# Three expert layers in batches of four blocks, two of them with the inverse root kept by token columns

## The chip, the cores and the metric

The kernel runs on one core of a Trainium2 chip, alone. The metric is the device time of one execution in microseconds (us). The engines are named as in the profile: PE is the matrix engine (PEld is its weight loads), DVE the vector engine, ACT the scalar engine, POOL is GpSimd, and SP is the engine whose queue issues the DMAs here.

## The reference, cut to what matters

Four layers, each a mixing step followed by a mixture of experts with a residual. The mixing steps (attention, similarity, a state-space scan, involution) are outside the change. The expert step of the first and the third layer is, for the tokens `t` of 64 channels (8 images of 1024 tokens), with two experts a token (`TOP_K = 2`):

```python
t = t + _L0_ffn_ref(_ln_t(t), ...)          # _ln_t: (v - mean) / sqrt(var + 1e-5) over the channels
...
gate_logits = xf @ Wg + bg                  # xf: the tokens, normalised; 8 experts
top_w, top_i = jax.lax.top_k(gate_logits, TOP_K)
top_w = jax.nn.softmax(top_w, axis=-1)
w_dense = jnp.sum(jax.nn.one_hot(top_i, E, dtype=xf.dtype) * top_w[..., None], axis=1)
for e in range(E):
    h = jax.nn.gelu(xf @ W1[e] + b1[e], approximate=False)
    out = out + w_dense[:, e:e + 1] * (h @ W2[e] + b2[e])
```

In the first, third and fourth layer (the last one) W1 is 64x256 and W2 256x64 for each expert; in the second layer the hidden size is 128. Everything is float32. All experts are computed for all tokens, and the gates that are 0 take out what isn't wanted.

## The kernel before

**Layout.** Images go in pairs: the 128 partitions hold 64 channels of two images, the columns 4 x 1024 tokens. `X` is the residual. A tile is 512 of these columns, so an expert step has `NT = 8` tiles, and it is one program block that begins when all engines have left the block before. `HIDDEN` gives 2 blocks of 128 hidden units per expert in layers L0, L2 and L3 and 1 in L1; so a tile has 16 blocks in those three. `experts("L0")` and `experts("L2")` have `norms=1` (the layer norm is made inside), `experts("L3")` has `norms=0` (the normalised input and the router's input come by DMA), and so has L1.

**A block on PE.** `up(t, k, b)` (L654) is two matmuls, one for each image half: 64 rows of weights by 128 columns, 512 tokens. The two use different row halves of the array. ACT then makes `Gelu` of both halves in one instruction (L734). `down(b)` (L666) is two matmuls of 128 rows by 64 columns into the two partition halves of one PSUM bank; the two blocks of an expert accumulate. The trace shows each float32 matmul as two records, with two weight loads.

**The order.** In a round PE goes up for two blocks and then down for the two blocks before them: 8 rounds a tile. Four PSUM banks take what goes up, two (4 and 5) the experts' outputs in turn, and bank `SIDE = 7` takes the preparation of the next tile. DVE adds the bias and multiplies each expert's output by its gate row `WB` (L869), POOL adds the eight up (L585), and DVE folds the sum into `X` (L877).

**Preparation of the next tile** runs beside these rounds, at places given by the tables `pe_at`, `act_at` and `dve_at`. For `norms=1`: PE centers the tile (L604), DVE copies it to `CEN` (L768), ACT squares it (L704), PE averages the squares over channels, one matmul that leaves the variance repeated on all rows (L610). DVE then finds the inverse root on all 512 columns, by an integer guess (L778, L780) and three Newton steps of three instructions (L784 to L786), and multiplies `CEN` by it (L789). PE forms the logits from the normalised tile, four matmuls with 128 tokens as the weights and 16 output columns (L620). DVE ranks them (L797 to L811), ACT bends the difference (L712), DVE makes the gates (L830 to L834), PE turns them (L630), ACT copies the rows (L719), and SP writes them to DRAM (L547) and reads them back repeated over the partitions into `WB` (L555). The first tile of a layer has no rounds to run beside: there the whole chain stands ahead.

On PE and ACT, six of the eight tiles are run by a hardware loop and the last two are written out; DVE has the same loop, POOL loops over all eight.

## Time and profile before

| | before |
|---|---|
| time, median of 3 runs | 2050.46 us (2049.69 to 2051.26) |
| the profiled execution | 2050.83 us |
| its span, first to last instruction | 2049.0 us |
| PE busy | 1743.1 us, 85% of the span |
| DVE busy | 1056.1 us, 52% |
| ACT busy | 887.8 us, 43% |
| POOL busy | 517.9 us, 25% |

The expert blocks of the three layers lie, by the records of their first and last instructions, at about 153.8 to 446.7 us (L0), 1302.0 to 1597.0 us (L2) and 1769.1 to 2036.9 us (L3). In a timeline, records that follow each other and are alike are merged into one row with their count. The end of a matmul is modelled, so the start of the next row tells more of PE's pace than a row's own length. The number behind "PEclk" is the granted TensorE clock as a share of 2.4 GHz.

### The profile page before, as it was taken

To read this page: it belongs to the slowest core of one execution; us is meant where nothing else is said; L and a number is where in the kernel's file an instruction comes from. 1 tells how busy PE (TensorE), PEld (TensorE's weight loads), DVE (VectorE), ACT (ScalarE), POOL (GpSimd) and SP (SyncE) were. 2 spreads that over 40 slices of the span, in tenths; PEclk is the share of its full clock that TensorE was granted. 3 is DMA by queue.
4 is the path that set the end of the run, shared out by engine and by line. 5 is a ranking of instruction groups with operands and counts; after the bars stand their busy time and mean duration, and the time that the engine had idled before them with its cause. 6 is when DMAs were issued, how large, how long until landed. Compare 5 with 4: busy or idle time off the path is not lost. (4 is left out here: it accounts for less than half of the span.)

```text
span 2049.0 us, 51344 instructions
## 1 busy us (share of the span) xinstructions
PE 1743.1 (85%) x20852; PEld 761.9 (37%) x20852; DVE 1056.1 (52%) x2060; ACT 887.8 (43%) x1134; POOL 517.9 (25%) x692
## 2 busy tenths in 40 slices
PE   5777999997999788887688887699999587699997
PEld 2442333333433222233477773233333233233332
DVE  2446575733555466440276773576765276243341
ACT  3213555553435344443344434355555500555553
POOL 0001232320000134420266560122222155022222
PEclk8998999997999899998899997799999898799998
DMA  6001313110000344336433422023222030223323
GB/s 225 12 10 42 84 42 83 42 42 31 11 0 1 88 110 105 73 114 220 165 104 100 128 73 93 22 62 71 54 62 64 0 41 1 62 69 88 92 64 83
DMA packets 62287, 145.08 MB, mean 71 GB/s; under 512 B 35240, under 2 KB 35240, under 8 KB 57984
## 3 DMA queue, kind: packets, MB, share of 16 engines
q1 hardware_dynamic: 62208, 144.12, 26.3%
q8 instruction: 38, 0.62, 0.1%
q14 instruction: 41, 0.34, 0.1%
HBM read 106.07 MB, written 25.44 MB: 64 GB/s over the span
## 5 line engine op out<-in xcount | busy, mean ns | idle before, releaser
L734 ACT ACTIVATE ARENA<-PS,W 128x1024 f32<-128x1024 f32 x448 | 474.8, 1109 | 332.6 <-PE PS L654 332.3
L585 POOL TENSOR_TENSOR ARENA<-ARENA 128x512 f32<-128x512 f32 x224 | 293.0, 1308 | 1176.5 <-DVE ARENA L869 1173.3
L654 PE MATMUL PS<-ARENA,W 64*128 64x512 f32 x1792 | 463.2, 637 | 0.8 <-ACT ARENA L734 0.8
L666 PE MATMUL PS<-ARENA,W 128*64 128x512 f32 x1792 | 433.7, 605 | 12.1 <-DVE ARENA L869 12.1
L869 DVE SCALAR_TENSOR_TENSOR ARENA<-PS,W,ARENA 128x512 f32<-128x512 f32 x256 | 190.4, 750 | 341.5 <-PE PS L666 280.5
L654 PEld LDWEIGHTS PS<-ARENA,W 64*128 64x128 f32 x1792 | 160.0, 193 | 262.0 <-issue 152.7
L666 PEld LDWEIGHTS PS<-ARENA,W 128*64 128x64 f32 x1792 | 108.9, 136 | 301.9 <-issue 207.3
L1769 PE MATMUL PS<-ARENA 32*32 32x32 f32 x8448 | 106.4, 196 | 6.3 <-issue 5.9
L1246 DVE TENSOR_TENSOR ARENA<-ARENA 128x1024 f32<-128x1024 f32 x64 | 75.5, 1221 | 69.3 <-PE PS L1179 36.1
L1216 ACT ACTIVATE ARENA<-PS 128x1024 f32<-128x1024 f32 x64 | 62.0, 1021 | 93.1 <-PE PS L1169 93.1
L1769 PEld LDWEIGHTS PS<-ARENA 32*32 32x32 f32 x8448 | 95.3, 105 | 10.5 <-issue 7.1
L2000 PE MATMUL PS<-ARENA,W 128*128 x144 | 73.3, 657 | 22.2 <-DVE ARENA L2027 15.1
L1636 ACT ACTIVATE ARENA<-PS 128x512 f32<-128x512 f32 x64 | 38.2, 597 | 108.1 <-PE PS L1743 108.1
L1169 PE MATMUL PS<-ARENA 64*128 64x512 f32 x256 | 74.6, 656 | 9.1 <-DVE ARENA L1237 4.7
L1396 PE MATMUL PS<-XN,ARENA 64*128 64x512 f32 (+2 forms) x288 | 67.8, 627 | 16.7 <-ACT ARENA L1427 14.1
L1179 PE MATMUL PS<-ARENA 128*64 128x512 f32 x256 | 73.8, 606 | 4.1 <-DVE ARENA L1246 4.1
L2051 POOL TENSOR_TENSOR ARENA<-ARENA 128x512 f32<-128x512 f32 x40 | 56.4, 1411 | 58.3 <-DVE ARENA L2027 56.4
L1668 DVE STREAM_TRANSPOSE ARENA<-ARENA 128x256 f32<-128x256 f32 x64 | 28.0, 438 | 83.4 <-PEq L1336 80.3
L620 PE MATMUL PS<-W,ARENA 128*128 128x16 f32 x256 | 37.7, 281 | 34.8 <-DVE ARENA L789 18.1
L342 PE MATMUL PS<-X,W 128*128 128x512 f32 x80 | 42.7, 639 | 28.6 <-PEq L296 16.0
L1699 DVE TENSOR_TENSOR ARENA<-ARENA,PS 128x512 f32<-128x512 f32 x64 | 43.9, 686 | 41.0 <-PE PS L1769 40.6
L785 DVE SCALAR_TENSOR_TENSOR ARENA<-ARENA 128x512 f32<-128x512 f32 x48 | 59.7, 1244 | 1.6
(216 smaller groups left out, 2096.4 us busy)
## 6 DMA issues: line engine op xcount, KB each, us to landing
ARENA<-scratch_g SPq DMA_DIRECT2D x64, 768.0 KB, 9.7
ARENA<-scratch_g SPq DMA_DIRECT2D x64, 256.0 KB, 3.9
W<-w_dram SPq DMA_DIRECT2D x1, 7307.5 KB, 30.0
ARENA<-XN SPq DMA_DIRECT2D x12, 512.0 KB, 3.5
ARENA<-XN SPq DMA_DIRECT2D x16, 256.0 KB, 2.3
scratch_x<-ARENA SPq DMA_DIRECT2D x8, 512.0 KB, 4.2
scratch_b<-ARENA SPq DMA_DIRECT2D x8, 512.0 KB, 3.2
scratch_z<-ARENA SPq DMA_DIRECT2D x8, 512.0 KB, 3.8
```

The lines of the kernel that those rows point to most:

```text
L585: nc.gpsimd.tensor_tensor(SUM[:, k, :], SUM[:, k, :], TMP[:, e % 2, :], ALU.add)\
L654: last = mm(PS[:, (b % 2) * R + r, :], w(layer + "_w1", b * 128, (b + 1) * 128, half(r)), XE[half(r), k, :], start=True, stop=True)
L666: last = mm(PS[half(r), 4 + e % 2, :], w(layer + "_w2", b * C, (b + 1) * C), H[:, b % 4, r * T:(r + 1) * T], start=part == 0, stop=part == ...
L734: f(H[:, b % 4, :], PS[:, (b % 2) * R:(b % 2) * R + R, :].rearrange("p a b -> p (a b)"), ACT.Gelu, bias=w(layer + "_b1", b, b + 1)).then_i ...
L869: v.scalar_tensor_tensor(TMP[:, e % 2, :] if e else SUM[:, k, :], PS[:, 4 + e % 2, :], w(layer + "_b2", e, e + 1), WB[:, k, e, :], ALU.add ...
L1169: last = mm(PS[:, 2 * r + h, :], XH[half(r), k, m * TOK:(m + 1) * TOK], XH[half(r), k, h * T:(h + 1) * T], start=True, stop=True)
L1179: last = mm(PS[half(r), 6 + h, :], TT[k][:, r, m, :], R2[:, r, h * T:(h + 1) * T], start=m == 0, stop=m == JS - 1)
L1216: nc.scalar.activation(RL[:, r, :], both(2 * r), ACT.Relu).then_inc(s_relu.sem, 1)
L1246: v.tensor_tensor(R2[:, r, :], RL[:, r, :], RL[:, r, :], ALU.mult)\
L1396: last = mm(PS[:, 4 * (u % 2) + 2 * r + h, skip:], wt, XN[half(r), q * S + h * T + skip - back:q * S + (h + 1) * T - back], start=tap == T ...
L1769: last = mm(PS[g, MIX + k, t], XD[g, k, j, u * CHUNK:(u + 1) * CHUNK], M[g, k, u * P + j * CHUNK:u * P + (j + 1) * CHUNK], start=u == 0, s ...
L2000: nc.tensor.matmul(PS[:, n % 6, :], w("i_ws", tap * P, (tap + 1) * P), RN[:, bass.ds(q * S + h * T, T)], start=True, stop=True)\
```

## The change

`deep_experts` takes the place of `experts` in L0, L2 and L3. L1 keeps the old function. What it does otherwise:

- **Batches.** PE goes up for four blocks, then down for the four before them: 4 rounds a tile. Three pairs of PSUM banks take what goes up (`UPS = 3`), so the fourth block of a batch waits for the `Gelu` of the first. `H` has six places (`HS = 6`), so the third and fourth `Gelu` of a batch wait for an expert's output of the batch before.
- **Banks.** The other two banks are shared in turn by the experts' outputs and the preparation's steps, in the order of the list `order`; `out_of` gives the bank, and `behind` and `emptied` the wait for the one that had it before.
- **Logits.** In L0 and L2 they are formed from the centered tile `CEN`, before it is scaled (L1043), and multiplied by the inverse root on DVE (L1226), with the bias added after (L1228).
- **Inverse root.** The squares are averaged with 128 tokens as the weights and two output columns, four matmuls (L1050), so that the variance stands as 128x8. All of the root's instructions are 128x8. ACT spreads it to 128x512 (`widen`, L1150), and PE turns it to rows by the identity, four matmuls of 128x128 (`scale`, L1058). DVE multiplies `CEN` by that out of PSUM (L1233).
- **Start.** In the first tile PE goes up for four blocks, not two, ahead of the turn of the gates.
- **No loop on PE and ACT.** All eight tiles are written out there. DVE's and POOL's loops are as before. The gates' rows lie in another buffer.

```diff
+        def deep_experts(layer, norms=1, router=None):
...
+            BAT, UPS, HS = 4, 3, 6
+            XS, H = a.take(2, T), a.take(HS, R * T)
...
+            RT = ROWS[:, 0:2 * T].rearrange("p (k t) -> p k t", k=2)
...
+            VAR, INV, NEWT = (a.take(GR) for _ in range(3))
+            WIDE = a.take(G, P)
...
+                order = ["center", 0, 1, "logits", 2, 3, "scale", 4, 5, "turn", 6, 7]
+                after_scale = {0: 0, 2: 2, 4: 4, 6: 6, "center": -1, "logits": 1, "scale": 3, "turn": 5}
+                at_last = {3: 1, 5: 3, 7: 5}
+                pe_at = {0: "center", 0.5: "logits", 2: "scale", 3: "turn"}
+                act_at = {(0, 1): "square", (1, 1): "widen", (2, 1): "bend", (3, 1): "rows"}
+                dve_at = {-1: "keep", 1: "invert", 3: "rank norm", 4: "weigh"}
+            else:
+                order = [0, 1, "logits", 2, 3, 4, 5, "turn", 6, 7]
...
+                pe_at = {1: "logits", 3: "turn"}
+                act_at = {(1, 3): "bend", (3, 1): "rows"}
+                dve_at = {1: "rank", 3: "weigh"}
+
+            def out_of(unit):
+
+                return UPS * R + order.index(unit) % 2
...
+                            for g in range(G):
+                                last = mm(PS[:, out_of("logits"), GR * E + g * R:GR * E + (g + 1) * R],
+                                          SQ[:, g * TOK:(g + 1) * TOK], w("mean64")[:, 0:P:C], start=True, stop=True)
+                            last.then_inc(ln_varied.sem, 1)
+
+                    def scale(p):
+                        behind("scale", p - 1)
+                        pe.wait_ge(ln_log.sem, ln_log.at(p + 1))
+                        for g in range(G):
+                            last = mm(PS[:, out_of("scale"), g * TOK:(g + 1) * TOK],
+                                      WIDE[:, g, :], w("ident"), start=True, stop=True)
+                        last.then_inc(ln_scaled.sem, 1)
...
+                        if u >= UPS:
+                            pe.wait_ge(e_gelu.sem, e_gelu.at(u - UPS + 1))
...
+                        elif norms and e == 5:
+                            pe.wait_ge(ln_normed.sem, ln_normed.at(t + 2))
...
+                    for t in range(NT):
+                        for n in range(NBAT):
+                            for u in range(t * NB + (n + 1) * BAT, t * NB + (n + 2) * BAT):
+                                if u < NT * NB:
+                                    up(u)
+                            if t + 1 < NT:
+                                prepare(pe_at.get(n), t + 1)
+                            for b in range(n * BAT, (n + 1) * BAT):
+                                down(t, b)
...
+                        f(WIDE.rearrange("p g (r c) -> p (g r) c", r=R), INV.unsqueeze(2).to_broadcast([P, GR, C]),
+                          ACT.Copy).then_inc(ln_log.sem, 1)
...
+                        if u >= HS:
+                            act.wait_ge(e_out.sem, e_out.at((u - HS) // blocks + 1))
...
-        experts("L0")
+        deep_experts("L0")
...
-        experts("L2")
+        deep_experts("L2")
...
-        experts("L3", norms=0, router=once)
+        deep_experts("L3", norms=0, router=once)
```

PE in L0, before, the start of a looped tile: L654 goes up, L666 down, L604 centers, L610 averages the squares. `x2` counts two instructions in a row.

```order
 L604 MATMUL PS<-X,W 128x512
 L663 ISA
 L666 MATMUL PS<-ARENA,W 64x512 [waits e_gelu,e_scaled]
 L666 MATMUL PS<-ARENA,W 64x512
 L666 MATMUL PS<-ARENA,W 64x512 [waits e_gelu]
 L666 MATMUL PS<-ARENA,W 64x512
 L652 REGISTER_ALU
 L654 MATMUL PS<-ARENA,W 128x512 [waits e_gelu]
 L654 MATMUL PS<-ARENA,W 128x512
```

There are four matmuls (two blocks) between one change of kind and the next.

PE in L0, after, the third batch of the first tile: L1087 goes up (the last block of four is shown), L1058 is `scale`, L1115 goes down.

```order
 L1087 MATMUL PS<-ARENA,W 128x512 [waits e_gelu]
 L1087 MATMUL PS<-ARENA,W 128x512
 L1058 MATMUL PS<-W,ARENA 128x128 [waits ln_log,e_scaled]
 L1058 MATMUL PS<-W,ARENA 128x128 x3
 L1115 MATMUL PS<-ARENA,W 64x512 [waits e_gelu,e_scaled]
 L1115 MATMUL PS<-ARENA,W 64x512
 L1115 MATMUL PS<-ARENA,W 64x512 [waits e_gelu]
 L1115 MATMUL PS<-ARENA,W 64x512
 L1115 MATMUL PS<-ARENA,W 64x512 [waits e_gelu,ln_normed]
 L1115 MATMUL PS<-ARENA,W 64x512
 L1115 MATMUL PS<-ARENA,W 64x512 [waits e_gelu]
 L1115 MATMUL PS<-ARENA,W 64x512
```

There are eight matmuls of a kind in a row, the turned root stands between the batches, and the sixth expert (its first matmul waits for `ln_normed`) stands behind DVE's reading of it.

DVE in L0, after, the chain ahead of the first tile (rows of the ranking left out): L1204 copies the centered tile, L1211 to L1220 find the root, L1226 and L1228 take the logits, L1249 begins the ranking, L1256 ends it, L1233 is the normalised tile.

```order
 L1204 COPY ARENA<-PS 128x512 [waits ln_centered]
 L1211 TENSOR_SCALAR ARENA<-PS,W 128x8 [waits ln_varied]
 L1214 TENSOR_SCALAR ARENA<-ARENA 128x8 [waits ln_taken]
 L1215 TENSOR_SCALAR ARENA<-ARENA 128x8 [waits ln_newton]
 L1218 TENSOR_TENSOR ARENA<-ARENA 128x8 [waits ln_newton]
 L1219 SCALAR_TENSOR_TENSOR ARENA<-ARENA 128x8 [waits ln_newton]
...
 L1226 TENSOR_TENSOR ARENA<-PS,ARENA 128x64 [waits g_logits,ln_newton]
 L1228 TENSOR_TENSOR ARENA<-ARENA,W 128x64 [waits g_chain]
...
 L1256 TENSOR_TENSOR ARENA<-ARENA 128x8 [waits g_chain]
 L1233 TENSOR_TENSOR ARENA<-PS,ARENA 128x512 [waits g_chain,ln_scaled]
 L1265 TENSOR_SCALAR ARENA<-ARENA 128x8 [waits g_bent]
```

Before, the root's twelve instructions here were 128x512, and the normalised tile came ahead of the logits and the ranking; now it comes after the ranking.

## Rows read from the trace of the kernel before

**Rows 1.** Busy time by stretch, L0: PE, PEld, DVE, ACT, POOL; then PEclk, DMA

```profile
211.40:383.60 172.20, 172.15 (x742) 58.30 (x740) 116.21 (x205) 91.82 (x96) 47.65 (x35) 1.00 0.28 62
```

**Rows 2.** Timeline of PE, L0, one looped tile: start, length, line and work

```profile
279.70 1.13 PE L604 MATMUL PS<-X,W 128*128 x2
280.75 1.94 PE L666 MATMUL PS<-ARENA,W 128*64 128x512 f32 x8
282.62 1.99 PE L654 MATMUL PS<-ARENA,W 64*128 64x512 f32 x8
284.54 1.13 PE L610 MATMUL PS<-ARENA,W 128*128 128x512 f32 x2
...
298.82 1.06 PE L620 MATMUL PS<-W,ARENA 128*128 128x16 f32 x8
299.81 1.99 PE L654 MATMUL PS<-ARENA,W 64*128 64x512 f32 x8
...
307.45 1.05 PE L630 MATMUL PS<-W,ARENA 128*16 128x128 f32 x8
```

**Rows 3.** Timeline of PE, the end of L0: four blocks down in a row

```profile
440.12 3.65 PE L666 MATMUL PS<-ARENA,W 128*64 128x512 f32 x16
```

**Rows 4.** Timeline of DVE, L0: the folds of a looped and a written-out tile

```profile
383.64 0.69 DVE L877 TENSOR_TENSOR X<-X,ARENA 128x512 f32 x1 [1.57 <-POOL ARENA L585]
417.81 0.69 DVE L877 TENSOR_TENSOR X<-X,ARENA 128x512 f32<-128x512 f32 x1 [1.46 <-POOL ARENA L585]
```

**Rows 5.** Timeline of PE, linear attention: 128 weight columns, 64 moving

```profile
66.78 1.11 PE L994 MATMUL PS<-W,ARENA 128*128 128x64 f32 x8
```

**Rows 6.** Timeline of ACT, L0: two Gelus behind the up at 282.62

```profile
283.80 2.12 ACT L734 ACTIVATE ARENA<-PS,W 128x1024 f32<-128x1024 f32 x2 [1.53 <-PE PS L654]
```

**Rows 7.** Timeline of DVE, L0: one instruction of the ranking, beside POOL's addition

```profile
300.43 1.28 DVE L803 TENSOR_TENSOR ARENA<-ARENA 128x64 f32<-128x64 f32 x1
```

**Rows 8.** Timeline of PE, the start of L0

```profile
153.80 1.10 PE L604 MATMUL PS<-X,W 128*128 128x512 f32 x2 [1.12 <-PEq L920]
...
168.31 3.79 PE L654 MATMUL PS<-ARENA,W 64*128 64x512 f32 x8
173.29 1.05 PE L630 MATMUL PS<-W,ARENA 128*16 128x128 f32 x8 [1.19 <-DVEq L836]
```

**Rows 9.** Timeline of DVE, the start of L0

```profile
154.94 0.69 DVE L768 COPY ARENA<-PS 128x512 f32<-128x512 f32 x1 [1.46 <-PE PS L604]
...
168.68 0.22 DVE L802 TENSOR_REDUCE ARENA<-ARENA 128x8 f32<-128x64 f32 x1
...
171.51 0.17 DVE L811 TENSOR_TENSOR ARENA<-ARENA 128x8 f32<-128x8 f32 x1
172.02 0.17 DVE L830 TENSOR_SCALAR ARENA<-ARENA 128x8 f32<-128x8 f32 x1 [0.34 <-ACT ARENA L712]
172.23 0.17 DVE L831 TENSOR_SCALAR ARENA<-ARENA 128x8 f32<-128x8 f32 x1
...
181.53 0.75 DVE L869 SCALAR_TENSOR_TENSOR ARENA<-PS,W,ARENA 128x512 f32<-128x512 f32 x1 [3.49 <-DMA ARENA<-scratch_g]
```

**Rows 10.** Busy time by stretch, starts of L0 and L2, to read the PEclk

```profile
159.00:160.00 1.00, 0.00 (x0) 0.00 (x0) 0.93 (x3) 0.00 (x0) 0.00 (x0) 0.50 0.00 0
172.00:173.00 1.00, 0.10 (x2) 0.00 (x0) 0.84 (x5) 1.00 (x2) 0.00 (x0) 0.80 0.00 0
...
1326.00:1327.00 1.00, 1.00 (x5) 0.30 (x2) 0.00 (x0) 0.85 (x2) 0.00 (x0) 0.95 0.05 20
```

**Rows 11.** Timeline of PE, the start of L2: the turn

```profile
1321.53 1.89 PE L630 MATMUL PS<-W,ARENA 128*16 128x128 f32 x8 [1.19 <-DVEq L836]
```

**Rows 12.** Timeline of PE, the start of L3: the turn

```profile
1775.86 1.89 PE L630 MATMUL PS<-W,ARENA 128*16 128x128 f32 x8 [1.19 <-DVEq L836]
```

**Rows 13.** Timeline of DVE, L3: the third expert of the first tile

```profile
1793.46 0.75 DVE L869 SCALAR_TENSOR_TENSOR ARENA<-PS,W,ARENA 128x512 f32<-128x512 f32 x1 [5.06 <-DMA ARENA<-scratch_g]
```

**Rows 14.** DMA issues, 150 to 260 us: count, KB each, median us to landing

```profile
scratch_g<-ARENA SPq DMA_DIRECT2D x3, 32.0 KB, 1.6
```

317 lines of the change are left out of this document (added).

## The prediction

> **What bounds the kernel now.** I read the busy time by stretch first. In L0's steady part PE is busy for 172.15 of 172.20 us at the full clock, while DVE has 116 and ACT 92 [rows 1]. So a tile costs what PE issues in it. L2 and L3 show the same picture. A faster root on DVE is worth nothing there by itself; what PE does is what counts, and DVE counts only at a layer's start, where nothing runs beside its chain.
>
> The timeline of PE gives the price list, taken from one row's start to the next [rows 2]. Two blocks down take 282.62 - 280.75 = 1.87 us. Two blocks up take 284.54 - 282.62 = 1.92. Centering takes 1.05, the average of squares is as long a row (1.13) and so takes 1.05, the logits 299.81 - 298.82 = 0.99, and the turn, as long as the logits less 0.01, 0.98. A round is 3.79, and a tile is 8 x 3.79 + 1.05 + 1.05 + 0.99 + 0.98 = 34.39 us. In L3, without the two norm steps, it is 32.29.
>
> Then one row at the end of L0, where nothing is left to go up: four blocks down in a row are 3.65 us long, and a row of two is 1.94 [rows 2, 3]. So two blocks behind others of their kind cost 1.71. The rest, 0.16 down and 1.92 - 1.71 = 0.21 up, is paid for each change of kind on PE. This is the time that the batches attack.
>
> **The rounds (gain 35.5 us).** In a layer there are 64 pairs of blocks up and 64 down. In batches of four, 32 pairs of each direction stand behind a pair of their kind: 32 x 0.21 + 32 x 0.16 = 11.8 us (the pair that already did so at the end stays). Three layers give 35.5 us. A batch round is then 2 x (3.79 - 0.185) = 7.21 us.
>
> **PE's steps beside them (loss 11.5 us).** In L0 and L2, for each of 7 tiles that are prepared beside rounds:
> - the average of squares goes: -1.05;
> - eight-record group of variance matmuls comes, with 128 weight columns and 2 moving ones. The logits' group has the same weights and 16 moving columns and takes 0.99 [rows 2]. It stands directly behind the logits, so one change of kind (0.16) is not paid again: +0.83;
> - the turned root comes, four float32 matmuls with 128 weight columns and 128 moving. No row of before has both. From below, the turn with 16 weight columns takes 0.98. A row with 128 weight columns and 64 moving is 1.11 long, or 1.04 without the 0.07 by which rows overrun the next start [rows 2, 5]. From above, were the load not hidden behind the stream at all, each of 8 records would cost up to 0.99/8 = 0.12 more, 2.0 in all. I take 1.04, since that row has half the stream and the full load and shows no sum of the two.
>
> The net is +0.82 a tile, 14 tiles, 11.5 us. A tile of L0 or L2 is then 4 x 7.21 + 1.05 + 0.99 + 0.83 + 1.04 + 0.98 = 33.7 us, against 34.4. A tile of L3 is 28.84 + 0.99 + 0.98 = 30.8, against 32.3.
>
> On that last term the Trainium skill speaks against the change: "TensorE: Matmul & The Clock Gate", section "Part 3: Packing small matmuls — row/col tiling", says that a weight load overlaps a running matmul only where its row group differs. All eight records of the turned root use all rows, so by that rule the term is 2.0 and not 1.04. That is a rival below.
>
> **The start of L0 (gain 2.8).** Before, the centering starts at 153.80 and the turn of the gates at 173.29, with two blocks up behind it [rows 8]. Now, by the same rows: `CEN` is there at 154.94 + 0.69 = 155.63 [rows 9]. Logits and then variances follow on PE (0.99 + 0.83) to 157.6, with ACT's squares hidden beside the logits. Twelve instructions of 128x8 at 0.21 (172.23 - 172.02) take 2.5, and two of 128x64 for the logits 0.5: 160.8. The twelve of the ranking stay 3.0 (168.68 to 171.68): 163.8. The normalised tile comes only then, 0.7: 164.5. ACT's spreading and PE's turned root fit under the ranking. Four blocks up follow. Two took 3.79 at half the clock [rows 8]; four take 3.79 + 3.42 - 0.1 = 7.1, so the turn starts at about 171.7. The gates (1.2 us of DVE from 164.5) are long done. That is 1.6 us earlier, with one pair more behind it, worth 1.71: 3.3 us.
>
> The clock takes some of it. It fell to 0.50 in the idle of the root and rose again around 172.2, before the turn [rows 10]. The turn now starts before that moment, 0.5 us of it at half: 2.8 remain. If the clock does not fall in the shorter idle (4 us and 2 us instead of 9), the four blocks take 3.6 and 3.5 us more are gained, in each of L0 and L2. If it rises 3 us later, 1.5 are lost.
>
> **The starts of L2 (gain 2.5) and L3 (gain 0.9).** L2 is the same chain, but there the turn itself ran at half the clock, 1.89, and the clock rose only at about 1326.05 [rows 10, 11]. With the turn 1.6 us earlier that much more runs at half: 3.3 - 0.8. In L3 the logits chain does not change, and the first two blocks up were hidden behind the ranking; four are 7.1 us, from 1770.9 to 1778.0, where the turn started at 1775.86 [rows 12]. That is -2.1, +1.71 for the pair, and +1.3 since less work at half the clock is left behind the turn.
>
> **What the gates' trip does.** The first scaling waited for the DMA until 181.53, 6.5 us behind the rows of gates, and in L3 the third expert's until 1793.46, 15.1 us behind them [rows 9, 13]. Both are measured from the turn, which moves by -1.6 and +2.1. Behind the turn PE now has 3.6 (up) + 1.05 + 1.8 before the first output and 3.6 + 1.05 + 3.6 before the logits, the first step that waits for the first scaling. In L0 that is 172.9 + 8.3 = 181.2 against 173.7 + 6.5 + 0.75 = 181.0. It just fits; if it does not, it is some tenths, once a layer.
>
> **The new waits, at nothing.** (a) The fourth block up waits for the first's `Gelu`. A `Gelu` starts 283.80 - 282.62 = 1.18 us after the batch and is 1.11 long [rows 2, 6]: 2.29, and the fourth block starts at 0.2 + 3 x 0.855 = 2.77. Cover 0.5 us, less the semaphore. Behind that wait on PE stand the whole preparation and the downs. (b) `Gelu`s three and four wait for an output of the batch before; they end 2.4 us after it, and the block that needs the fourth starts 1.7 + 0.2 + 1.7 = 3.6 after it. (c) The sixth expert waits for the normalised tile. From the end of the fourth expert: DVE scales it (0.9), ranks (3.0), loses about 1.05 where POOL's addition holds one instruction (0.22 becomes 1.28 [rows 7]) and normalises (0.75): 5.7 to 5.9. PE: 3.6 + 1.04 + 1.71 = 6.4. Cover 0.5. (d) Written-out code: the fold of the first written-out tile comes 34.17 us after the one before [rows 4], no slower than the 34.39 of the sum, so it costs nothing there, on either engine.
>
> **Sum.** 35.5 - 11.5 + 2.8 + 2.5 + 0.9 = 30.2 us. The profiled execution took 2050.83 us (span 2049.0 and 1.8 around it), 0.4 above the median of 2050.46. So 2050.46 - 30.2 = 2020.3 us. What follows each layer (DVE's last two scalings, POOL's addition, the fold) is as it was.
>
> **The rivals.**
> - *The weight load of the turned root is not hidden* (chance 0.10). 8 x 0.12 = 0.97 in each of 16 tiles: +15.5, 2036 us. For it speaks that no row has a full load and a full stream in this width; against it, rows 5.
> - *New waits in each batch* (0.15). If (a) or (c) falls short, PE stops in most of the 96 batches. A quarter of a microsecond each is +24: 2044 us. From 0.3 us each on, nothing is left of the gain. For it: two covers of 0.5 us are thin. Against: the second block down waits for a `Gelu` now, and the rows keep their 1.94.
> - *The change of kind is not what costs* (0.03). Were the 0.16 and 0.21 a price of each pair's first matmul that comes in batches too, the rounds would give nothing and the added steps would show: 2050.5 + 11.5 - 6.2 = 2056 us, slower. Rows 3 speaks against it, for down; for up it is carried over.
> - *The fetch of PE's written-out code* (0.05). All 24 tiles' code comes once, and nothing is looped. The nearest row for a small transfer is 1.6 us to landing [rows 14]. At one exposed fetch a tile it is +38 and at two +77; it decides from about 19 exposed fetches on. At one: 2059 us, slower. Against: rows 4.
> - *A warm start* (0.05): 2 x 3.5 us more, 2013 us.
>
> **How the numbers follow.** My forecast has 0.62, and its own range is 2014 to 2027 (the clock, and a tenth of a microsecond in each batch). The range given reaches to the warm start and the unhidden load: 2010 to 2037. Outside lie most of the waits, the fetch and the change that gives nothing, 2 in 10. This kernel can tell about 0.2%, 4.1 us, from no change. Faster by more: the forecast, the warm start, the unhidden load and most of the waits, 0.89. Within: 0.03, the heavier end of the waits. Slower: 0.08.
>
> **What would show it.** The profile of after should have PE full at clock 1.00 in the three layers, tiles 33.7 us apart in L0 and L2 and 30.8 in L3, rows of 16 records 3.65 (down) and 3.70 (up) long, the turned root's row 1.1 long (2.0 under the first rival), the new variance group 0.83 behind the logits, and the turn 17.9 us after the centering in L0. Idle of PE put down to L1180 (`Gelu`) or L1233 inside tiles would show the second rival, and idle put down to the queue or to nothing at a tile's start the fetch. Wrong would be the whole sum if the tiles' distance doesn't fall.

## Result and the profile after

| | before | after |
|---|---|---|
| median | 2050.86 us (2049.69 to 2055.36, 4 runs) | 2018.24 us (2014.10 to 2025.59, 4 runs) |
| ratio to before | | 0.9847 (0.9813 to 0.9881) |
| span of the profiled run | 2049.0 us | 2013.4 us |
| PE busy | 1743.1 us | 1720.9 us |
| DVE busy | 1056.1 us | 941.5 us |

The kernel became 32.6 us faster; 30.2 had been forecast. The interval of the ratio is 24.4 to 38.4 us, so the whole times alone could not tell the two numbers apart. In a later set of runs (`after_again`) the same kernel took 2015.56 us (6 runs, ratio 0.9824, 0.9796 to 0.9852). The whole times of one kernel spread by 10 us and more (before: 2042.17 to 2062.71 in 25 runs on one chip), so the comparisons below use lengths inside the layers as well: from the first matmul of L0, L2 or L3 to the start of its last fold. In the two profiles of the changed kernel (`after` and `after_again`) these are 283.18 and 285.20 us (L0), 284.21 and 282.98 (L2), 253.71 and 253.58 (L3). The differences in L0 and L2 arise ahead of the first fold (53.99 against 56.00, and 55.02 against 53.78), and they come with the granted clock: see the section on the start of a layer.

| layer | before | after | difference | forecast |
|---|---|---|---|---|
| L0 | 292.22 | 283.18 | -9.04 | -8.9 |
| L2 | 294.29 | 284.21 | -10.08 | -8.6 |
| L3 | 267.15 | 253.71 | -13.44 | -12.7 |
| the three | 853.66 | 821.10 | -32.56 | -30.2 |

The rest of the profiled span, 3.0 us of the 35.6, comes from parts that the change does not touch; in L1, for one, the eight folds spread over 147.1 us before and 144.8 after.

Busy time by stretch, after, in the steady parts of L0, L2 and L3 (PE, PEld, DVE, ACT, POOL, then PEclk, DMA share, GB/s). These answer [rows 1]:

```profile
212.00:378.00 166.00, 166.00 (x802) 68.34 (x800) 78.76 (x209) 92.91 (x99) 44.23 (x35) 1.00 0.27 61
1379.00:1548.00 169.00, 169.00 (x810) 69.35 (x810) 79.88 (x210) 94.01 (x100) 44.60 (x35) 1.00 0.28 63
1789.00:1974.00 185.00, 185.00 (x866) 70.40 (x864) 72.34 (x162) 105.58 (x109) 53.32 (x43) 1.00 0.35 84
```

PE is full at the full clock, as before. DVE fell from 0.67 of the time to 0.47 and gained the kernel nothing by that, inside the tiles. The timeline of PE over one tile of L0, after, answers [rows 2] (L1087 goes up, L1115 down, L1058 turns the root, L1066 the gates, L1033 centers, L1043 and L1050 are logits and variances):

```profile
282.82 1.06 PE L1043 MATMUL PS<-W,ARENA 128*128 128x16 f32 x8
283.73 1.03 PE L1050 MATMUL PS<-W,ARENA 128*128 128x2 f32 x8
284.69 3.70 PE L1087 MATMUL PS<-ARENA,W 64*128 64x512 f32 x16
288.33 3.65 PE L1115 MATMUL PS<-ARENA,W 128*64 128x512 f32 x16
291.91 3.71 PE L1087 MATMUL PS<-ARENA,W 64*128 64x512 f32 x16
295.55 1.16 PE L1058 MATMUL PS<-W,ARENA 128*128 128x128 f32 x8
296.64 3.65 PE L1115 MATMUL PS<-ARENA,W 128*64 128x512 f32 x16
300.22 3.70 PE L1087 MATMUL PS<-ARENA,W 64*128 64x512 f32 x16
303.86 1.05 PE L1066 MATMUL PS<-W,ARENA 128*16 128x128 f32 x8
304.83 3.65 PE L1115 MATMUL PS<-ARENA,W 128*64 128x512 f32 x16
308.42 3.70 PE L1087 MATMUL PS<-ARENA,W 64*128 64x512 f32 x16
312.05 1.12 PE L1033 MATMUL PS<-X,W 128*128 128x512 f32 x2
313.11 3.65 PE L1115 MATMUL PS<-ARENA,W 128*64 128x512 f32 x16
316.69 1.06 PE L1043 MATMUL PS<-W,ARENA 128*128 128x16 f32 x8
```

No row has an idle bracket. Four blocks take 3.64 up and 3.58 down (start to start), the root 1.09, the two 128-column groups together 284.69 - 282.82 = 1.87. The folds of two tiles, which answer [rows 4]:

```profile
344.82 0.69 DVE L1310 TENSOR_TENSOR X<-X,ARENA 128x512 f32 x1 [1.58 <-POOL ARENA L1014]
378.70 0.69 DVE L1310 TENSOR_TENSOR X<-X,ARENA 128x512 f32 x1 [1.58 <-POOL ARENA L1014]
```

They are 33.88 us apart; 33.7 was forecast. In L3 the distance is 30.85, forecast 30.8. At the end of L0, which answers [rows 3], stands something that was not in the forecast:

```profile
432.62 3.65 PE L1115 MATMUL PS<-ARENA,W 128*64 128x512 f32 x16 [0.85 <-DVE ARENA L1302]
```

In the last tile nothing goes up between the last two batches down, and the sixth and the seventh expert have the same bank, since the turn's place between them is empty. The seventh waits for DVE. From 428.11, where the batch before begins, to 432.62 are 4.51 us; four blocks down behind others of their kind would take 3.42 by the prediction's 1.71, so the loss is 1.09.

### The profile page after: what moved, and what is told of

The parts are those of the page before. It is cut to its first block and busy times, and to the rows that moved or that the text cites. A ratio compares the mean times of both kernels' runs of the same rounds, so it can differ in the third digit from the quotient of the medians.

```text
span 2013.4 us, 51379 instructions
## 1 busy us (share of the span) xinstructions
PE 1720.9 (85%) x21076; PEld 805.2 (40%) x21076; DVE 941.5 (47%) x2076; ACT 896.1 (45%) x1150; POOL 510.4 (25%) x692
## 5 line engine op out<-in xcount | busy, mean ns | idle before, releaser
L1014 POOL TENSOR_TENSOR ARENA<-ARENA 128x512 f32<-128x512 f32 x168 | 214.3, 1275 | 809.3 <-DVE ARENA L1302 808.7
L1087 PE MATMUL PS<-ARENA,W 64*128 64x512 f32 x1536 | 363.7, 613 | 3.3 <-DVE ARENA L1233 3.3
L1115 PE MATMUL PS<-ARENA,W 128*64 128x512 f32 x1536 | 350.8, 599 | 2.6 <-DVE ARENA L1302 2.6
L1087 PEld LDWEIGHTS PS<-ARENA,W 64*128 64x128 f32 x1536 | 143.0, 190 | 207.3 <-issue 108.2
L1115 PEld LDWEIGHTS PS<-ARENA,W 128*64 128x64 f32 x1536 | 101.8, 136 | 214.6 <-issue 206.8
L585 POOL TENSOR_TENSOR ARENA<-ARENA 128x512 f32<-128x512 f32 x56 | 70.9, 1267 | 340.5 <-DVE ARENA L869 338.5
L1829 PE MATMUL PS<-XN,ARENA 64*128 64x512 f32 (+2 forms) x288 | 66.2, 613 | 15.2 <-ACT ARENA L1860 12.7
L666 PE MATMUL PS<-ARENA,W 128*64 128x512 f32 x256 | 62.8, 610 | 12.4 <-DVE ARENA L869 12.4
L2484 POOL TENSOR_TENSOR ARENA<-ARENA 128x512 f32<-128x512 f32 x40 | 56.3, 1408 | 58.3 <-DVE ARENA L2460 56.5
L654 PE MATMUL PS<-ARENA,W 64*128 64x512 f32 x256 | 70.9, 677 | 0.0
```

Of the source, the lines that this page charges most:

```text
L585: nc.gpsimd.tensor_tensor(SUM[:, k, :], SUM[:, k, :], TMP[:, e % 2, :], ALU.add)\
L654: last = mm(PS[:, (b % 2) * R + r, :], w(layer + "_w1", b * 128, (b + 1) * 128, half(r)), XE[half(r), k, :], start=True, stop=True)
L1014: nc.gpsimd.tensor_tensor(SUM[:, k, :], SUM[:, k, :], TMP[:, e % 2, :], ALU.add)\
L1087: last = mm(PS[:, (u % UPS) * R + r, :], w(layer + "_w1", b * 128, (b + 1) * 128, half(r)), XS[half(r), t % 2, :], start=True, stop=True)
L1115: last = mm(PS[half(r), out_of(e), :], w(layer + "_w2", b * C, (b + 1) * C), H[:, u % HS, r * T:(r + 1) * T], start=part == 0, stop=part = ...
```

## The experiments

Lengths are in us, by the measure above, each from one profile. Each ratio is taken against runs of the kernel before on the same chip. `kept_warm2` and `norm_first2` were run once each, so they are read from the lengths inside the layers alone. A difference of up to 2 us in L0 or L2 says nothing by itself, since `after` and `after_again` are the same kernel.

| kernel | L0 | L2 | L3 | sum | whole, median (runs) | ratio to before |
|---|---|---|---|---|---|---|
| before | 292.22 | 294.29 | 267.15 | 853.66 | 2050.86 (4) | 1 |
| after | 283.18 | 284.21 | 253.71 | 821.10 | 2018.24 (4) | 0.9847 |
| l3_alone | 292.23 | 294.20 | 253.74 | 840.17 | 2039.75 (10) | 0.9946 (0.9917 to 0.9974) |
| rounds_of_two | 293.32 | 294.32 | 266.15 | 853.79 | 2055.37 (10) | 1.0018 (0.9986 to 1.005) |
| root_turned_twice | 288.59 | 290.37 | 253.72 | 832.68 | 2029.92 (10) | 0.9913 (0.9882 to 0.9945) |
| root_by_rows | 286.51 | 285.01 | 252.62 | 824.14 | 2018.79 (4) | 0.9854 (0.9809 to 0.9899) |
| rows_placed2 | 281.83 | 281.86 | 252.56 | 816.25 | 2019.38 (4) | 0.985 (0.9803 to 0.9897) |
| kept_warm2 | 281.08 | 281.68 | 253.72 | 816.48 | 2021.67 (1) | |
| norm_first2 | 284.37 | 282.65 | 253.70 | 820.72 | 2020.35 (1) | |
| both2 | 275.76 | 276.85 | 252.60 | 805.21 | 2008.88 (6) | 0.9796 (0.9759 to 0.9833) |
| after_again | 285.20 | 282.98 | 253.58 | 821.76 | 2015.56 (6) | 0.9824 (0.9796 to 0.9852) |
| bend_second | 276.34 | 275.97 | 252.59 | 804.90 | 2004.24 (6) | 0.9764 (0.9737 to 0.9792) |

### The batches

`l3_alone`, on the changed kernel:

```diff
-        deep_experts("L0")
+        experts("L0")
-        deep_experts("L2")
+        experts("L2")
```

> Only the last expert layer (L3) uses the new function, the first and the third keep the old one; nothing of the column root is in it. Theory (the gain is the change of kind on PE, 0.37 us a pair of rounds merged): tiles of L3 30.86 us apart instead of 32.27, L0 and L2 unchanged at 34.4, the layer 12.7 to 13.4 us shorter, so about 2037 us. Rival (the gain needs the shorter DVE chain of the column root): L3 has no root, so little would be gained here, 2048 us or more.

L3 shrank by 13.41 us and its tiles stood 30.85 apart, while L0 and L2 kept their 292.2 and 294.2. L3 has no root and no shorter DVE chain. So the gain does not need them, and the rival is out, for this layer.

`rounds_of_two` undoes the batches alone:

```diff
-            BAT, UPS, HS = 4, 3, 6
+            BAT, UPS, HS = 2, 3, 6
-                pe_at = {0: "center", 0.5: "logits", 2: "scale", 3: "turn"}
-                act_at = {(0, 1): "square", (1, 1): "widen", (2, 1): "bend", (3, 1): "rows"}
+                pe_at = {0: "center", 1.5: "logits", 4: "scale", 6: "turn"}
+                act_at = {(1, 1): "square", (3, 1): "widen", (4, 1): "bend", (6, 1): "rows"}
...
-                pe_at = {1: "logits", 3: "turn"}
-                act_at = {(1, 3): "bend", (3, 1): "rows"}
+                pe_at = {2: "logits", 6: "turn"}
+                act_at = {(4, 1): "bend", (6, 1): "rows"}
```

> The changed kernel with batches of two blocks again: same banks, same six places in H, same column root, still written out on PE and ACT. Theory: each tile is 4 changes of kind each way dearer, 4 x 0.37 = 1.48 us: 35.3 us apart in L0 and L2 (dearer than before the change, 34.4), 32.3 in L3. That is 35.5 us in all, less some 1 to 2 us a layer because the turn of the gates no longer waits for four blocks up: 2048 to 2053 us, the time of the kernel before. Rival (the third pair of banks, the places in H or the missing loop give the gain): it stays near 2018.

The timeline of PE in L0 of this kernel:

```profile
278.58 1.94 PE L1115 MATMUL PS<-ARENA,W 128*64 128x512 f32 x8
280.45 1.99 PE L1087 MATMUL PS<-ARENA,W 64*128 64x512 f32 x8
282.37 1.94 PE L1115 MATMUL PS<-ARENA,W 128*64 128x512 f32 x8
```

Down takes 1.87 and up 1.92 again. Tiles stood 35.28 apart in L0 and L2, 1.41 above those of after, and 32.26 in L3, again 1.41. The three layers came to 853.79 us, which is before's 853.66 to a tenth. So without the batches the column root, the third pair of banks, the six places in `H` and the written-out code together bring nothing. That zero is a balance: a tile of L0 or L2 is 0.84 us dearer than before (35.28 against a mean of 34.44), while the first fold comes earlier by 4.0 us in L0, 5.1 in L2 and 1.0 in L3. For each pair merged in both directions 1.41 / 4 = 0.35 us are saved, where the forecast had 0.37.

### The root

`root_turned_twice` issues the turned root's matmuls twice:

```diff
-                        for g in range(G):
+                        for g in [*range(G), *range(G)]:
```

> The changed kernel, with the four matmuls that turn the root to rows issued twice in each tile of L0 and L2 (same result). Theory (PE has no idle, and a record with 128 weight columns and 128 moving columns costs 0.107 to 0.12 us, the load hidden behind the stream): +0.86 to +0.97 a tile, 16 tiles: +14 to +16 us. Rival of the weight load that is not hidden: 8 records of 0.21 or more, +1.7 to +1.9 a tile, +27 to +31. Rival of hidden work (PE has slack in these tiles): below +3.

```profile
295.97 2.05 PE L1058 MATMUL PS<-W,ARENA 128*128 128x128 f32 x16
297.95 3.65 PE L1115 MATMUL PS<-ARENA,W 128*64 128x512 f32 x16
```

The sixteen records take 1.98, against 1.09 for eight; 0.89 more, 0.11 a record. Tiles went from 33.87 to 34.77. So PE has no slack there. In `kept_warm2` below eight records of 512 columns take 3.52 us, 0.44 each, so 128 columns would take 0.11 (an estimate from these rows). That is all that a record here costs, so the load of its 128 weight columns is hidden behind the stream. The rule of the Trainium skill that the prediction weighed ("TensorE: Matmul & The Clock Gate", section "Part 3: Packing small matmuls — row/col tiling", a load overlaps only where the row group differs) does not hold for these records, which all use every row. The sum grew by 11.6 us and not by 14 to 16: the price is paid in the 14 tiles that are prepared beside rounds, 14 x 0.89 = 12.5. In a layer's first tile the extra matmuls made the blocks up start 0.8 us (L0) and 0.5 us (L2) later, but the clock had risen by then: the four blocks took 3.64 us instead of 5.88 and 6.63, and the turn came 1.4 and 2.5 us earlier. Waits of the logits, and in L2 a fall of the clock, took part of that again.

`root_by_rows` puts the root back to DVE's 512 columns, in batches of four, and swaps the last tile's last two banks:

```diff
-                order = ["center", 0, 1, "logits", 2, 3, "scale", 4, 5, "turn", 6, 7]
+                order = ["center", 0, 1, "vary", 2, 3, 4, 5, "logits", 6, 7, "turn"]
...
-                pe_at = {0: "center", 0.5: "logits", 2: "scale", 3: "turn"}
+                pe_at = {0: "center", 0.5: "vary", 2.5: "logits", 3.5: "turn"}
...
-                dve_at = {-1: "keep", 1: "invert", 3: "rank norm", 4: "weigh"}
+                dve_at = {-1: "keep", 1: "start 3", 2: "3", 3: "3 norm", 5: "rank weigh"}
```

> Batches of four kept, the root put back to 512 columns on DVE, one matmul for the averages and the logits from the normalised tile, as before the change. In the last tile the last two experts also swap banks, so that the last batch does not wait for DVE. Theory (PE's issue is the price of a tile): tile of L0 and L2 4 x 7.21 + 4.07 = 32.9 instead of 33.87, 14 tiles: -13.4; chain at the start of L0 and L2 about 5 us longer each: +10; the swap -0.9 in each of three layers: -2.8. Together -6: 2012 us. Rival (the long chain on DVE, some 9 us a tile and up to 1 us more for each addition of POOL, is late for a bank or for the next tile's blocks): tiles of 34 us or more, 2020 us or more.

The expectation failed, and its rival was half right: DVE was late, but most tiles stayed below the 34 us that it named. Five of the six tiles of L0 stood 33.3 to 33.7 apart, not 32.9, and one 35.7. PE and then DVE of this kernel, L0:

```profile
300.94 1.06 PE L1056 MATMUL PS<-W,ARENA 128*128 128x16 f32 x8 [0.65 <-DVE ARENA L1332]
```
```profile
289.18 0.69 DVE L1236 SCALAR_TENSOR_TENSOR ARENA<-ARENA 128x512 f32<-128x512 f32 x1
291.77 0.75 DVE L1332 SCALAR_TENSOR_TENSOR ARENA<-PS,W,ARENA 128x512 f32<-128x512 f32 x1 [1.90 <-DMA ARENA<-scratch_g]
```

DVE stood 1.9 us at the wait for the gates of the third expert, which come late because the turn now stands last in the tile, with two Newton steps queued behind that wait. The logits on PE then waited 0.65. The tile of 35.7 has a wait of 1.01 at the same place and, behind it, four blocks up that took 5.33 us at half the clock instead of 3.64:

```profile
369.29 5.40 PE L1103 MATMUL PS<-ARENA,W 64*128 64x512 f32 x16
371.00:372.00 1.00, 1.00 (x4) 0.43 (x4) 0.86 (x5) 1.00 (x1) 0.01 (x1) 0.50 0.00 0
```

That is the clock and not DVE's chain; such stretches come back in the next section. The swap did what was said of it: L3, which differs from after by nothing else, became 1.09 us shorter, and the last tile's distance went from 26.16 to 25.09.

`rows_placed2`, against `root_by_rows`, asks whether the chain is too long or badly placed:

```diff
-                order = ["center", 0, 1, "vary", 2, 3, 4, 5, "logits", 6, 7, "turn"]
+                order = ["center", 0, 1, "vary", 2, 3, "logits", 4, 5, "turn", 6, 7]
...
-                pe_at = {0: "center", 0.5: "vary", 2.5: "logits", 3.5: "turn"}
-                act_at = {(0, 1): "square", (3, 1): "bend", (3, 3): "rows"}
-                dve_at = {-1: "keep", 1: "start 3", 2: "3", 3: "3 norm", 5: "rank weigh"}
+                pe_at = {0: "center", 0.5: "vary", 2: "logits", 3: "turn"}
+                act_at = {(0, 1): "square", (2, 3): "bend", (3, 1): "rows"}
+                dve_at = {-1: "keep", 1: "start 3 3", 2: "3 norm", 3: "rank", 4: "weigh"}
```

> Batches of four with the root by rows on DVE as in root_by_rows, but the steps in the places that the column version has: two Newton steps ahead of the wait for the gates' DMA, the logits ahead of the fifth expert, the turn ahead of the seventh. Theory (root_by_rows lost its gain to late steps: DVE stood 1.9 us at the DMA wait of the third expert with Newton steps behind it, the logits came 0.65 us late): tiles of L0 and L2 at PE's sum, 4 x 7.21 + 4.07 = 32.9 us, without idle of PE; L0 54 + 3.7 for the longer start, 280.2 in all. Rival (DVE's chain is too long wherever it stands): tiles above 33.5 us.

It was placed badly, for the most part. The tiles came to 33.16 and 33.26 in L0; what is left above 32.9 is a wait of the logits for DVE:

```profile
297.42 1.04 PE L1056 MATMUL PS<-W,ARENA 128*128 128x16 f32 x8 [0.15 <-DVE ARENA L1245]
```

So the column root is the dearer one inside the tiles, by 0.6 to 0.7 us each. Where it earns is the start: the turn of the gates comes 16.61 us behind the centering in L0 after and 20.29 in this kernel, though both have four blocks up ahead of it. Over a whole layer the two nearly cancel: apart from the swap's 1.09 this kernel is 0.3 us shorter than after in L0 and 1.3 in L2, and level with L2 of `after_again`.

### The start of a layer

`kept_warm2` fills PE's idle ahead of the first tile of L0 and L2 with centering matmuls whose result nobody reads:

```diff
+                    def busy(n):
+                        for _ in range(n):
+                            mm(PS[:, 0, :], w("center"), tile(X, 0), start=True, stop=True)
...
                         if pe_at[n] == "turn":
+                            if norms:
+                                busy(2)
                             for u in range(BAT):
                                 up(u)
                         prepare(pe_at[n], 0)
+                        if pe_at[n] == "logits" and norms:
+                            busy(4)
```

> The changed kernel, with centering matmuls whose result nobody reads put into the idle of PE ahead of the first tile of L0 and L2: four behind the variances, two behind the turned root. Read from the trace, within the layers. Theory (the clock fell to 1.2 GHz in that idle and the four blocks up paid for it): clock 1.00 throughout, root turned in 1.1 us instead of 2.1, four blocks up 3.7 long instead of 5.94 (L0) and 6.69 (L2): turn of the gates 2.2 to 3 us earlier, L0 281.0 instead of 283.2 and L2 281.2 instead of 284.2. Rival (the chain on DVE and the DMA of the gates set the start): the four blocks are faster but the layers stay within 0.5 us of 283.2 and 284.2.

PE at the start of L0, after and then this kernel, and the clock of this kernel there (busy time by stretch):

```profile
155.34 1.10 PE L1033 MATMUL PS<-X,W 128*128 128x512 f32 x2 [1.12 <-PEq L1353]
...
162.35 2.08 PE L1058 MATMUL PS<-W,ARENA 128*128 128x128 f32 x8 [3.19 <-ACT ARENA L1150]
166.07 5.94 PE L1087 MATMUL PS<-ARENA,W 64*128 64x512 f32 x16 [1.64 <-DVE ARENA L1233]
171.95 1.05 PE L1066 MATMUL PS<-W,ARENA 128*16 128x128 f32 x8
```
```profile
154.94 1.10 PE L1033 MATMUL PS<-X,W 128*128 128x512 f32 x2 [1.11 <-PEq L1361]
...
158.63 3.68 PE L1122 MATMUL PS<-X,W 128*128 128x512 f32 x8
162.15 1.05 PE L1058 MATMUL PS<-W,ARENA 128*128 128x128 f32 x8
163.04 1.88 PE L1122 MATMUL PS<-X,W 128*128 128x512 f32 x4
165.69 3.70 PE L1087 MATMUL PS<-ARENA,W 64*128 64x512 f32 x16 [0.77 <-DVE ARENA L1241]
169.32 1.05 PE L1066 MATMUL PS<-W,ARENA 128*16 128x128 f32 x8
```
```profile
158.00:172.00 14.00, 13.23 (x59) 6.72 (x61) 6.75 (x32) 5.92 (x8) 0.00 (x0) 1.00 0.00 1
```

The blocks start at the same moment of the chain (10.73 and 10.75 us behind the centering) and take 3.63 instead of 5.88. The granted clock was 1.00 from 158 to 172 us here, and 0.50 from 161 to 170 in the changed kernel. The turn comes 14.4 us behind the centering in L0 and L2, against 16.61 and 17.64 in `after` and 16.35 in both layers of `after_again`. So the clock costs the start 1.9 to 3.2 us, and that is shown. The layers became 2.10 (L0) and 2.53 us (L2) shorter than in `after`. The expectation held in L0; in L2 it is missed by 0.5 us, and there the logits waited 0.63 us for the first scaling.

`norm_first2` makes the first tile's input ahead of the ranking:

```diff
                     for e in sorted(dve_at):
-                        prepare(dve_at[e])
+                        prepare("norm rank" if dve_at[e] == "rank norm" else dve_at[e])
```

> The changed kernel, with the first tile's normalised input made ahead of the ranking on DVE instead of behind it, in L0 and L2. Read from the trace. Theory (the four blocks up wait for DVE's ranking): the blocks can start when PE has turned the root (164.4 in the trace of after) plus 0.9 us, 0.8 us earlier than now, so each layer is 0.8 us shorter. Rival (the turn waits for the gates then): no change.

The blocks started 9.88 us behind the centering in both layers, 0.85 earlier in L0. L2 became 1.56 us shorter, but L0 1.19 longer. PE in L0 of this kernel, behind the first tile's logits, and the clock (busy time by stretch):

```profile
181.35 5.40 PE L1087 MATMUL PS<-ARENA,W 64*128 64x512 f32 x16
186.68 3.65 PE L1115 MATMUL PS<-ARENA,W 128*64 128x512 f32 x16
```
```profile
181.00:182.00 1.00, 1.00 (x8) 0.75 (x10) 0.47 (x3) 0.00 (x0) 0.64 (x1) 1.00 1.00 221
183.00:184.00 1.00, 1.00 (x6) 0.49 (x4) 0.77 (x5) 0.65 (x1) 0.00 (x0) 0.50 1.00 201
186.00:187.00 1.00, 1.00 (x6) 0.20 (x4) 0.00 (x0) 0.00 (x0) 0.00 (x0) 1.00 0.00 0
```

The clock fell to 1.2 GHz for some 3 us while PE's records have no gap, and four blocks took 5.33 instead of 3.64. That loss of 1.7 is why L0 did not become shorter. Ahead of the fall stood the two groups with 16 and 2 moving columns, as they do in each tile without such a fall.

The fall does not need this edit. The unchanged kernel has it too, in L0 of `after_again` at the same place, behind a wait of 0.50 us of the logits for DVE; there, too, four blocks took 5.33:

```profile
194.26 5.40 PE L1087 MATMUL PS<-ARENA,W 64*128 64x512 f32 x16
196.00:197.00 1.00, 1.00 (x6) 0.49 (x4) 0.74 (x6) 0.93 (x1) 0.00 (x0) 0.50 0.38 74
```

With that wait it makes up the 2 us by which L0 of `after_again` is longer than L0 of `after`. L2 of `root_turned_twice` has the fall behind a wait of 0.62 us, but L2 of `kept_warm2`, behind one of 0.63, does not. Why it falls in one place and not in the other stays open.

What the order itself is worth is less than 0.85 us. The turn came 15.9 us behind the centering, 0.7 earlier than in L0 of `after` and 0.4 earlier than in `after_again`, since more of the four blocks now ran at half the clock (6.03 us instead of 5.88). Most of the 1.56 us in L2 is the clock as well: in L2 of `after` it rose 17.1 us behind the centering, here 14.7.

### Both roots, each where it is cheaper

`both2` is `rows_placed2` with the column root for the first tile, where nothing hides the chain, its normalised input ahead of the ranking, and spare matmuls in PE's idle:

```diff
-            columns_first = norms and False
+            columns_first = norms and True
...
                         last.then_inc(ln_varied.sem, 1)
+                        busy(4)
                         pe.wait_ge(ln_log.sem, ln_log.at(1))
...
                         last.then_inc(ln_scaled.sem, 1)
+                        busy(1)
```

> rows_placed for the seven tiles that have rounds to run beside, the column root for the first tile alone, where nothing hides the chain, with its normalised input ahead of the ranking and PE kept busy in its idle (four and one spare centering matmuls), and the last two experts of a layer in swapped banks. Theory: each root where it is cheaper. Start to first fold 54.0 - 2.5 (clock) - 0.8 (order) - 0.9 (first prepared tile) = about 50 us in L0 and L2, tiles 32.9, last tile 25.1: L0 and L2 about 272.5 each, L3 252.6, together 23 us less than the changed kernel; about 1995 us. Rival (only parts of it add up, since the earlier turn runs into the gates' DMA): 2005 us or more.

The sum of the three layers is 805.21, 15.9 us below after and 48.5 below before; 23 had been expected. The parts: tiles at 33.2 and not 32.9, and 51.9 and 52.9 us to the first fold, not 50. PE there:

```profile
168.32 1.13 PE L1109 MATMUL PS<-ARENA,W 64*128 64x512 f32 x4 [1.35 <-ACT ARENA L1207]
```

The fourth block up waited for the first `Gelu`, and ACT stood at the bending of the gates, in front of that `Gelu`, until DVE had ranked. Behind it PE waited 0.83 us for the first scaling, which waits for the gates' DMA: the expectation's rival, in part. In L2 the clock also fell to half during the four spare matmuls (1286.5 to 1289.9 us), which took 5.21 us there and 3.52 in L0.

`bend_second` puts the bending behind the first `Gelu` of `both2`; `after_again` is the changed kernel, unchanged, on the same chip:

```diff
-                            for u in range(BAT):
+                            for u in range(int(bool(columns_first)), BAT):
                                 bend_up(u)
                         if columns_first and act_at[at] == "bend":
                             widen(0)
+                            bend_up(0)
```

> The changed kernel itself, to stand beside the next one on the same chip. The whole times of all kernels spread by some 10 us, the three changed layers by less than 0.5: 2012 to 2030 us, L0 283 to 284, L2 283 to 285, L3 253.7.

> The combined version (row root where rounds run beside, column root, normalised input first and PE kept busy in the first tile), with ACT's bending of the gates behind the first Gelu of the first tile and not ahead of it. In the combined version PE's fourth block up waited 1.35 us for that Gelu, since ACT stood at the bending until DVE had ranked. Theory: the turn comes 1.35 us earlier, and the layers L0 and L2 are up to 1.35 us shorter: 274.4 and 275.5. Rival (the trip of the gates through DRAM sets the pace behind the turn; PE already waited 0.83 us for the first scaling there): the trip moves with the turn, so the same gain; if it doesn't move with it, nothing is gained, 275.8 and 276.9.

The first expectation held for the whole time and for L3. L0 (285.20) missed its range by 1.2 us, by the fall of the clock told above, and L2 (282.98) lay at the edge of its own.

PE at the same place of `bend_second`, and the clock during the spare matmuls ahead of it:

```profile
157.38 5.38 PE L1063 MATMUL PS<-X,W 128*128 128x512 f32 x8
...
164.44 3.71 PE L1109 MATMUL PS<-ARENA,W 64*128 64x512 f32 x16
168.88 1.05 PE L1088 MATMUL PS<-W,ARENA 128*16 128x128 f32 x8 [0.73 <-DVEq L1303]
```
```profile
159.00:160.00 1.00, 1.00 (x2) 0.34 (x1) 0.83 (x6) 0.00 (x0) 0.00 (x0) 0.50 0.00 0
```

The wait for the `Gelu` is gone, but the turn now waits 0.73 us for DVE's gates. The three layers together are the same, 804.90 against 805.21 (L2 0.9 shorter, L0 0.6 longer). The two layers do not compare alike: during the spare matmuls the clock was at half for some 3 us in both layers here, and in `both2` only in L2. In L2, where both kernels have that fall, the turn came 0.8 us earlier and the layer is 0.9 shorter, less than the expected 1.35, because of the new wait. In L0 the later clock hides the gain. As a whole this version has the lowest median: 2004.24 us, ratio 0.9764 (0.9737 to 0.9792), beside the changed kernel's 0.9824 (0.9796 to 0.9852) on the same chip. The intervals of `bend_second` and `both2` overlap, so these runs do not rank the two.

## Why the prediction was right

The mechanism held; how near the total came is in part luck, since errors of opposite sign cancel. `rounds_of_two` measures what a tile gains by the batches (35.28 - 33.87 = 1.41 us) and what it pays for the root (35.28 - 34.44 = 0.84), and `root_by_rows` the loss at the end (1.09). The starts are what is then left of each layer's difference. The sum is that of the layers' lengths, 853.66 - 821.10; the terms are rounded.

| term of the sum | forecast | measured |
|---|---|---|
| the rounds | 35.5 | 24 x 1.41 = 33.8 |
| PE's steps beside them | -11.5 | 14 x -0.84 = -11.8 |
| the starts of L0, L2, L3 | 2.8 + 2.5 + 0.9 = 6.2 | 4.7 + 5.8 + 3.3 = 13.8 |
| the last tiles | 0 | 3 x -1.09 = -3.3 |
| sum | 30.2 | 32.6 |

The rows of after in which the clock rises, at the starts of L0 and L2 (the last number but two is the PEclk):

```profile
170.00:171.00 1.00, 1.00 (x6) 0.25 (x4) 0.00 (x0) 1.00 (x1) 0.00 (x0) 0.69 0.00 0
1307.00:1308.00 1.00, 1.00 (x6) 0.16 (x3) 0.00 (x0) 0.91 (x2) 0.00 (x0) 0.87 0.00 0
```

- **PE is the bound, and the change of kind its price.** Right, and shown by undoing it: `rounds_of_two` gives all of it back. The step from one row of 16 records at the end to 0.16 down and 0.21 up measured 0.35 together where 0.37 was said. The Trainium skill ("TensorEngine Tiling (Array Packing)", section "Key Properties") says that a change of tiling mode drains the engine. The rows here agree that a change costs time, 0.35 us there and back; that a drain is what takes it is not shown by any run.
- **PE's steps beside the rounds.** The net of +0.82 a tile was close: 1.87 for logits and variances against 1.82, 1.09 for the root against 1.04, and 0.84 in the tiles. The tile measured 33.87 against 33.7.
- **The turned root's load.** The value between the bounds was the right one, and `root_turned_twice` shows the rival false. That rival counted 16 tiles; only 14 have the root beside rounds.
- **The start.** This is the term that was mis-sized. DVE's chain was right to 0.1 us: the blocks up start 10.73 us behind the centering, where the working had 10.7 (some 0.35 of that stands in the working's times without a row: 155.63 + 1.82 is 157.45 and not 157.6, and 157.6 + 3.0 is 160.6 and not 160.8). The working let the clock rise at the moment at which it had risen before. It rose earlier behind the start of the layer in all three: 15.3 us against 18.6 (L0), 17.1 against 24.1 (L2) and 7.5 against 11.0 (L3). In all three, four blocks up without a gap now stand ahead of the turn, where two blocks and an idle of PE stood; no run isolates whether that is the reason. So four blocks took 5.88 us in L0 and 6.63 in L2, not 7.1, the turn came 16.61 us behind the centering in L0, not 17.9, and the turn and the blocks behind it ran at the full clock in all three layers. `kept_warm2` shows what more the clock holds.
- **The last tile.** A loss that the prediction lacked: 0.85 us of wait, 1.09 in all, in each of three layers. The sentence "what follows each layer is as it was" was right; it was the last batch that changed. It hid behind the start's larger gain.
- **The new waits at nothing.** Right inside the tiles: in part 5 of the page PE's idle ahead of L1087 is 3.3 us, the starts of L0 and L2, and ahead of L1115 2.6 us, the three last tiles. In `both2`, where ACT had something in front of the `Gelu`, the wait of the fourth block cost 1.35 us at once.
- **Written-out code.** No idle at a tile's start is left to it; the loads of instructions rose from 38 to 54 packets on one queue and from 41 to 45 on the other, in the page's part 3.

## What to carry to other kernels

When an engine is full, read the price of its steps from start to start, and look for the one place where the same work stands twice in a row: the difference is what a change of kind costs, and batching saves it. Before two variants are compared by a stage of some microseconds, compare the granted clock of that stage in both. Work taken off an engine that has slack is paid for on the engine that has none: the column root freed a fifth of DVE's time and cost PE 0.6 to 0.7 us a tile, and belongs only where its chain is exposed, at a layer's start. After a schedule is moved, read its last round too, where the steps that kept two users of a buffer apart are missing.

## What the runs showed of the hardware that was not expected

- The granted clock fell to 0.50 for some 3 us inside stretches in which PE's records have no gap. In `norm_first2` (182.6 to 186.0 us), `after_again` (194.6 to 198.0), L2 of `root_turned_twice` (1319.0 to 1322.4) and `root_by_rows` (369.7 to 373.2) four blocks took 5.33 instead of 3.64 us. In L0 and L2 of `bend_second` (158.2 to 161.6 and 1294.8 to 1298.2) and in L2 of `both2` (1286.5 to 1289.9) it fell during spare matmuls. What tells such stretches from others is open.
- The lengths of tiles repeat to 0.01 us between chips (33.87 in L0 of `after_again` and `kept_warm2`), while a layer's start moves by 2 us in the same kernel (53.99 and 56.00 in L0), with the clock, and whole runs of one kernel spread by 10 us. An effect of a few us in one layer is seen in the layers' lengths long before it is seen in the medians.
